# Graph network, edge stage: three gather places, four result places, scatters four groups behind, a loop of twelve turns, and an older-first order in the first turns

## The reference

```python
h = jnp.concatenate([n_embed[senders], n_embed[receivers]], axis=-1)
h = jnp.tanh(h @ W0 + b0)          # 512 -> 416
h = jnp.tanh(h @ W1 + b1)          # 416 -> 324
h = h @ W2 + b2                    # 324 -> 256
h = h * (e_embed @ Wg)             # 128 -> 256
return _segment_mean(h, senders, n_embed.shape[0])
```

## Time and profile before

| | |
|---|---|
| median of 3 runs | 3157.38 us |
| the profiled execution's own time | 3163.51 us |
| its span, first to last instruction | 3161.9 us |
| TensorE, matmuls | 3050.7 us busy, 96% |
| VectorE | 2156.2 us busy, 68% |
| ScalarE | 1558.9 us busy, 49% |
| GpSimd | 1372.1 us busy, 43% |
| gathers of p and of q | 416 each, a median of 3.2 us from issue to landing |
| granted TensorE clock, mean | 0.988 of full |

### The profile page before, as it was taken

How to read it: one execution, slowest core, us unless ns; L and a number is a source line. 1 busy time by engine, 2 the same in 40 slices (tenths; PEclk the granted TensorE clock), 3 DMA queues, 4 the chain that set the end, 5 groups by cost and what they waited for, 6 DMA issues and landing times. The chain is left out here.

```text
span 3161.9 us, 65361 instructions
## 1 busy us (share of the span) xinstructions
PE 3050.7 (96%) x17338; PEld 2445.7 (77%) x17340; DVE 2156.2 (68%) x5608; ACT 1558.9 (49%) x3158; POOL 1372.1 (43%) x1479
## 2 busy tenths in 40 slices
PE   7699999999999999999998889999999999999899
PEld 7588888888888888888886566667777888887676
DVE  7788888888888888888885777774655222246523
ACT  2466666666666666666664777771111111111344
POOL 2677777777777777777773211220000000000011
PEclk9899999999999999999999999999999999999999
DMA  5555555555555555555553888887556777778586
GB/s 175 170 164 162 161 165 164 164 164 162 162 164 164 164 164 163 165 163 164 164 163 117 262 262 267 276 276 234 171 183 192 231 220 225 218 231 260 99 127 99
DMA packets 298299, 584.82 MB, mean 185 GB/s; under 512 B 43361, under 2 KB 150842, under 8 KB 298234
## 3 DMA queue, kind: packets, MB, share of 16 engines
q1 hardware_dynamic: 180960, 280.20, 29.9%
q0 software_dynamic: 90416, 254.46, 29.2%
q10 hardware_dynamic: 26858, 49.32, 4.3%
HBM read 493.97 MB, written 110.32 MB: 191 GB/s over the span
## 5 line engine op out<-in xcount | busy, mean ns | idle before, releaser
L985 PE MATMUL bank<-parts,ring 128*128 128x512 f32 x2500 | 622.6, 398 | 4.0 <-DVE T_buf L1761 1.9
L985 PEld LDWEIGHTS bank<-parts,ring 128*128 128x128 f32 x2500 | 461.1, 189 | 104.7 <-issue 5.4
L620 POOL DMA_INDIRECT msgs<-rows_out,sidx x416 | 408.4, 982 | 152.0 <-issue 94.8
L613 POOL DMA_INDIRECT p_in<-p_tab,gidx x416 | 403.4, 970 | 138.7 <-issue 112.7
L613 POOL DMA_INDIRECT q_in<-q_tab,gidx x416 | 398.3, 958 | 126.8 <-issue 126.2
L675 PE MATMUL bank<-hidden1h,w1h 128*108 128x512 f32 x936 | 406.8, 435 | 2.3 <-DVE hidden2l L865 2.3
L675 PE MATMUL bank<-w2h,hidden2h 108*128 108x256 f32 x1248 | 402.1, 322 | 0.0
L676 PE MATMUL bank<-hidden1l,w1h 128*108 128x512 f32 x936 | 369.0, 394 | 0.0
L677 PE MATMUL bank<-hidden1h,w1l 128*108 128x512 f32 x936 | 367.7, 393 | 0.0
L784 ACT ACTIVATE hidden2h<-bank,b1c 108x512 fp32r<-108x512 f32 (+1 forms) x312 | 214.5, 688 | 297.8 <-PE bank L691 297.8
L677 PE MATMUL bank<-w2h,hidden2l 108*128 108x256 f32 x1248 | 351.0, 281 | 0.0
(11 more groups left out here) (253 smaller groups left out, 5858.3 us busy)
## 6 DMA issues: line engine op xcount, KB each, us to landing
ring<-counts SPq DMA_DIRECT2D x500, 320.0 KB, 3.4
R_buf<-msgs SPq DMA_DIRECT2D x544, 130.0 KB, 3.1
counts<-cells ACTq DMA_DIRECT2D x125, 320.0 KB, 3.3
eT<-in_edge_T SPq DMA_DIRECT2D x104, 256.0 KB, 2.9
R_buf<-counts POOLq DMA_DIRECT2D x25, 480.0 KB, 6.8
R_buf<-counts POOLq DMA_DIRECT2D x25, 320.0 KB, 5.8
p_in<-p_tab,gidx POOLq DMA_INDIRECT x416, 3.2
q_in<-q_tab,gidx POOLq DMA_INDIRECT x416, 3.2
```

The source lines that it names most:

```text
L613: pool.indirect_dma_start(out=rows_in[:, z, c], out_offset=None, in_=tab[:], in_offset=bass.IndirectOffsetOnAxis(ap=gidx[:, z, which, c:c ...
L620: pool.indirect_dma_start(out=msgs[:], in_=rows_out[:, z, c], in_offset=None, out_offset=bass.IndirectOffsetOnAxis(ap=sidx[:, z, c:c + 1], ...
L985: mm = pe.matmul(bU[t].rearrange("p (w c) -> p w c", w=2), ring[:, cell(odd, a), t * P:(t + 1) * P].bitcast(dt), parts[k % 2][:, :, a].bit ...
```

## The change

There are three places for gathered rows and their indices (`INS`), four for result rows and theirs (`OUTS`), with `Turn.place` and `Turn.out` to count them. GpSimd's scatters are of group t-4 instead of t-2 (`LAG`). In the turns before turn 0 each chunk's q gather is issued right behind its p gather. The scatters of a place share one semaphore. The loop's body holds twelve turns (`ROUND`), the least number that two, three and four divide; the loops run 8 times on TensorE, ScalarE, GpSimd and SyncE and 7 times on VectorE, where they ran 50 times on TensorE and ScalarE, 48 on VectorE and GpSimd and 51 on SyncE.

The first turns have orders of their own. On TensorE and ScalarE turn 0 takes a step of group 0 ahead of each of group 1, and turns 1 and 2 take the steps of the older group first. On VectorE the turns up to turn 0 are written out step by step, and turns 1 and 2 have an order with messages and low parts first, adds last. From turn 3 on the order is the old one.

```diff
+OUTS, INS, ROUND = 4, 3, 12
-            p_in, q_in = (esb(n, [P, 2, GC, H1]) for n in ("p_in", "q_in"))
+            p_in, q_in = (esb(n, [P, INS, GC, H1]) for n in ("p_in", "q_in"))
-            rows_out = esb("rows_out", [P, 2, GC, RW])
+            rows_out = esb("rows_out", [P, OUTS, GC, RW])
...
                 def group(self, k):
-                    return 2 * self.it + (self.a + k)
+                    return ROUND * self.it + (self.a + k)
...
+            def filling(t):
+                return isinstance(t.it, int) and t.group(0) < 0
+            def early(t):
+                return isinstance(t.it, int) and 0 < t.group(0) < 3
...
-                with eng.Fori(0, (tail - head) // 2) as it:
-                    for u in range(2):
+                with eng.Fori(0, (tail - head) // ROUND) as it:
+                    for u in range(ROUND):
                         body(Turn(it, head + u))
...
+                LAG = 4
...
                     if t.has(3):
                         pool.wait_ge(s_idx, t.group(3) + 1)
-                        wait(pool, s_add, (t.group(3) - 1) * GC)
+                        wait(pool, s_add, (t.group(3) - INS + 1) * GC)
                         stand_alone(pool, s_up)
                         for c in range(GC):
                             gather(t, c, p_tab, 0, p_in)
+                            if filling(t):
+                                gather(t, c, q_tab, 1, q_in)
...
-                    if t.has(-2):
-                        pool.wait_ge(s_place, t.group(-2) + 1)
+                    if t.has(-LAG):
+                        pool.wait_ge(s_place, t.group(-LAG) + 1)
...
-                edge_loop(pool, body, -3, 4, G - 4, G + 2)
+                edge_loop(pool, body, -3, LAG, G - 4, G + LAG)
...
+                def first_turn(t):
+                    for m in range(H2T):
+                        first(t, m)
+                        transposes(t, m)
+                    transposes(t, H2T)
+
+                def early_turn(t):
+                    second(t, 0)
+                    places_before(t)
+                    second(t, 1)
+                    first(t, 0)
+                    transposes(t, 0)
+                    second(t, 2)
+                    first(t, 1)
+                    transposes(t, 1)
+                    second(t, 3)
+                    transposes(t, 2)
+                    first(t, 2)
+                    transposes(t, 3)
+                    places_after(t)
...
-                edge_loop(pe, body, -1, 3, G - 1, G + 1)
+                edge_loop(pe, body, -1, 3, G - 5, G + 1)
...
-                edge_loop(act, body, -1, 3, G - 1, G + 1)
+                edge_loop(act, body, -1, 3, G - 5, G + 1)
...
-                    for c in range(GC):
-                        wait(v, s_sc[z][c], 16 * t.use(-1))
+                    o = t.out(-1)
+                    wait(v, s_sc[o], 16 * GC * t.out_use(-1))
...
+                def first_turns():
+                    a, b, t = Turn(0, -2), Turn(0, -1), Turn(0, 0)
+                    add(a, 0)
+                    add(a, 1)
+                    first_low(b, 0)
+                    add(a, 2)
+                    first_low(b, 1)
+                    add(a, 3)
+                    first_low(b, 2)
+                    first_low(b, 3)
+                    add(b, 0)
+                    one_hots(t)
...
+                def early_turn(t):
+                    message(t, 0)
+                    places(t)
+                    message(t, 1)
+                    one_hots(t)
+                    second_low(t, 0)
+                    first_low(t, 0)
+                    message(t, 2)
+                    second_low(t, 1)
+                    first_low(t, 1)
+                    add(t, 0)
+                    message(t, 3)
+                    add(t, 1)
+                    first_low(t, 2)
+                    add(t, 2)
+                    second_low(t, 2)
+                    first_low(t, 3)
+                    add(t, 3)
...
-                edge_loop(v, body, -2, 3, G - 5, G + 1)
+                first_turns()
+                edge_loop(v, body, 1, 14, G - 6, G + 1)
```

More of the change, by code:

```diff
@@ L617, in scatter @@
                 def scatter(t, c):
[L619 to L622, removed]
+                    o = t.out(-LAG)
+                    pool.indirect_dma_start(out=msgs[:], in_=rows_out[:, o, c], in_offset=None,
+                                            out_offset=bass.IndirectOffsetOnAxis(ap=sidx[:, o, c:c + 1], axis=0)
+                                            ).then_inc(s_sc[o], 16)
                 def body(t):
-                    if t.has(-2) and t.has(1):
+                    if t.has(-2) and t.has(3):
                         pool.wait_ge(s_L2, t.group(-2) * GC + 3)
@@ L737, in _ @@
                 pe.wait_ge(s_one, 3)
+                def first_turn(t):
[17 more added lines that the diff above has]
+                    places_after(t)
                 def body(t):
+                    if isinstance(t.it, int) and t.group(0) == 0:
+                        return first_turn(t)
+                    if early(t):
+                        return early_turn(t)
                     transposes(t, 0)
@@ L796, in gate_out, with first_turn @@
                     act.copy(gate[:, c], bO[c % 2][:, D:2 * D]).then_inc(s_gt, 1)
+                def first_turn(t):
+                    for m in range(H2T):
+                        second_tanh(t, m)
+                        first_tanh(t, m)
+                    first_tanh(t, H2T)
+                def early_turn(t):
+                    gate_out(t, 0)
+                    gate_out(t, 1)
+                    second_tanh(t, 0)
+                    first_tanh(t, 0)
+                    gate_out(t, 2)
+                    second_tanh(t, 1)
+                    first_tanh(t, 1)
+                    gate_out(t, 3)
+                    first_tanh(t, 2)
+                    second_tanh(t, 2)
+                    first_tanh(t, 3)
                 def body(t):
+                    if isinstance(t.it, int) and t.group(0) == 0:
+                        return first_turn(t)
+                    if early(t):
+                        return early_turn(t)
                     first_tanh(t, 0)
@@ L903, in message, with early_turn @@
                     v.wait_ge(s_gt, j * GC + c + 1)
-                    v.tensor_tensor(rows_out[:, z, c, 0:D], bO[c % 2][:, 0:D], gate[:, c],
+                    v.tensor_tensor(rows_out[:, t.out(-1), c, 0:D], bO[c % 2][:, 0:D], gate[:, c],
                                     ALU.mult).then_inc(s_msg, 1)
+                def first_turns():
[10 more added lines that the diff above has]
+                    one_hots(t)
+                    add(b, 1)
+                    second_low(t, 0)
+                    first_low(t, 0)
+                    add(b, 2)
+                    second_low(t, 1)
+                    add(b, 3)
+                    first_low(t, 1)
[3 more added lines that the diff above has]
+                    first_low(t, 3)
+                    for c in range(1, GC):
+                        add(t, c)
+                def early_turn(t):
+                    message(t, 0)
+                    places(t)
+                    message(t, 1)
+                    one_hots(t)
+                    second_low(t, 0)
+                    first_low(t, 0)
+                    message(t, 2)
+                    second_low(t, 1)
+                    first_low(t, 1)
+                    add(t, 0)
+                    message(t, 3)
+                    add(t, 1)
+                    first_low(t, 2)
+                    add(t, 2)
+                    second_low(t, 2)
+                    first_low(t, 3)
+                    add(t, 3)
                 def body(t):
+                    if early(t):
+                        return early_turn(t)
                     one_hots(t)
@@ L931, in weights_low @@
                     v.tensor_tensor(w2l[:].bitcast(F32R), w2[:], w2h[:], ALU.subtract)
-                for z in range(2):
+                for z in range(INS):
                     table_rows(z, z)
```

59 lines of the change are left out of this document (33 added, 26 removed).

## The result

The changed kernel takes 3204.6 us (median of 5 runs, 3200.9 to 3209.7), the kernel before beside it 3156.6 us (3152.4 to 3157.7): ratio 1.0155, 95% interval 1.0144 to 1.0166. It is slower, as forecast, but by 48 us and not by 10.5. The two profiled executions stand 37.4 us apart (3163.5 and 3200.9 us); before's lies above all five of its runs here, 6.9 us over their median, and the changed kernel's is the lowest of its own, 3.7 us under. The three differences add up to the 48 us.

What follows compares the result with a forecast made beforehand. The prediction took TensorE's own work as the bound, with GpSimd just beside it. Its terms -0.6 -0.3 -3.9 +12.3 +3 gave +10.5 us on 3157.4, so 3168 us, range 3150 to 3184.

Steps and rivals of the forecast that it cites:

- The other engines' loops: Closing the longer loops on VectorE, ScalarE and the other engines besides TensorE: taken as +3 us, bounds 0 to +25 us.
- TensorE's miss: TensorE's seven closing branches take 3.85 us each for code fetch, 1.75 us of it uncovered: +12.3 us (0 to +15).
- The 49 closings: In the middle of the stage, 49 loop closings, each about 0.07 us longer than a plain turn, go away: -3.9 us.
- The first turns: Group 0's products start 4 us earlier, new waits give it back, turn 3 ends 0.3 us earlier: -0.3 us.
- Places and lag: More places and later scatters gain 0 in the middle; at the end the last scatter goes at once: -0.6 us.
- GpSimd's drift: GpSimd falls 0.04 us a turn behind TensorE, 4 us over 100 turns; its lead of about 8 us covers that.
- rival 2: VectorE and ScalarE miss as well, so the loop of twelve is dear on three engines: 3183 us; chance 0.12.
- Rival 3: GpSimd becomes the bound through misses of its own in the loop: another +10 us, 3178 us; chance 0.05.
- Rival 1: The long loop body stays resident or is fetched ahead, a small gain: 3152.6 us (3148.6 to 3156); chance 0.28.

## Why the prediction was wrong

- **The failed step is "The other engines' loops", above all "I take +3 us".** The bounds said 0 to +25, with 12 us for VectorE alone if it missed; the trace has 23.7 us for VectorE alone, and ScalarE idles 2.5 to 3.1 us in TensorE's closing turns. I placed it near the free end because branches of 0.06 us and a body of 527 rows looked harmless beside TensorE's 1022. The branch record says nothing on VectorE, and a body less than half as long missed. The price of one, too, was low: 3.0 us got through and not 2, since the third transpose waits for exactly the low part behind the stall, and then came what I had used at the first turns and not here: the clock falls behind such a wait, 1.9 us more.
- **TensorE's miss** was right: 3.7 to 4.1 us a branch against 3.85, code packets over 100, seven turns. Of it 2.0 to 2.3 us got through six times, 3.6 once, with a fall of the clock, not 1.75: +16.5 us against +12.3. ScalarE alone costs 2.4 us in the same turn; in the changed kernel the two overlap.
- **The 49 closings, -3.9 us,** did not come: plain turns are 15.25 and 15.27 us, not 15.21. It is not the first turns' order (they alone leave 15.23), so it goes with the places, the lag or where the buffers lie; that stays open. And where plain turns did get to 15.23, GpSimd took the gain back and more.
- **The first turns** came nearly as told. From the stage's first gather on, group 0's first product starts 4.4 us earlier (4 forecast), and turn 3 ends 0.2 us earlier (0.3). It starts at 114.12 us and not at 116.5, of which 2.0 us are the stage's earlier beginning. Waits of 2.3 us before turn 2 and of 0.7 and 1.7 us in turn 3 took much of that back (2.6 less some overlap, and 2.9, forecast). Against the other traces of the old order even the 0.2 us are not sure.
- **Places and lag** gained nothing in the middle of this comparison, as forecast, and nothing at the end: last message at 1751.02, its scatter at 1752.26 us, the 1.24 us of before; the -0.6 us were wrong. That the lead covers GpSimd's drift was true only because each second turn was 15.30 us long: the 8 us are the gathers' lead, but what ran out in the later runs, after some 5 us, was the scatters'.
- **The rivals:** rival 2 (VectorE and ScalarE miss as well) is what happened, at twice its price. It had 0.12. Rival 3 had GpSimd as the bound through misses of its own, and it has none; but as the bound it meets every version above that has no long turns. Rival 1 needed a body that stays resident; its low end should read 3148.9 us, since the 4 us of the first turns take the place of the 0.3.

## What to carry to other kernels

Before a loop body is made longer, look up how many instructions each engine's body will have, not TensorE's alone, and keep every one below what a loop has been seen to hold; a branch that looks short on VectorE or ScalarE can have 4 us behind it, found as idle time put down to issue. Price a stall by the first consumer that waits and add what the clock loses behind that wait. And where the next engine stands within 1% of the bound, removing 0.04 us a turn can use up its lead, and here the kernel became slower by it. Before a few us are called a gain, look whether both traces enter the stage at the same time.

## What the runs showed of the hardware

- Closings cost TensorE 3.7 to 4.6 us in the branch (2 us of it hidden), VectorE 3.3 to 4.4 us and ScalarE 2.4 to 3.1 us behind it. GpSimd with 244 instructions does not miss.
- In a run of twelve turns TensorE's code is fetched anew: three packets within 11 us of the jump, then one in about 18 us; VectorE's two or three within 8 us, then one in about 38 us. Written out in a line, VectorE's code came at a packet in about 50 us without a stall.
- GpSimd's issues of p gathers take 0.98 us while it is ahead and 1.02 us once it is the bound (rows above), those of q gathers 0.97 and 1.00 us, those of scatters 0.98 in both, so that turns jump from 15.27 to 15.6 us. Why they get longer is not shown.
